# An attention and feed-forward kernel on one core: x loaded tile by tile behind its stores, and the work of heads 7 to 15 placed anew

## What is computed

```python
xn = layernorm(x)
q, k, v = (xn @ W + b for W, b in ((Wq, bq), (Wk, bk), (Wv, bv)))      # split into 16 heads
scores = q @ k.T / sqrt(32) + slope[head] * distances                  # causal
ctx = softmax(scores) @ v
gate, up = xn @ gate_w.T, xn @ up_w.T
out = x + ctx @ Wo + bo + (silu(gate) * up) @ down_w.T
```

## Time and profile before

| | |
|---|---|
| median of 3 runs | 791.17 us (789.69 to 795.04) |
| profiled execution | 789.27 us |
| its span, first to last instruction | 787.4 us |
| mean granted TensorE clock | 0.947 |
| busy: PE, DVE, ACT, POOL | 87%, 58%, 57%, 42% |
| attention part | about the first 475 us |

### The profile page before, as it was taken

The page is one execution under the profiler, slowest core; times in us unless marked ns, Lnnn a source line. Parts: engine busy times, 40 slices in busy tenths (PEclk is TensorE's granted clock), DMA queues, the critical chain, the costliest instruction groups (busy, mean ns, idle before and its releaser), DMA issues. The chain is left out here.

```text
span 787.4 us, 13689 instructions
## 1 busy us (share of the span) xinstructions
PE 686.6 (87%) x4884; PEld 550.2 (70%) x4884; DVE 459.0 (58%) x1290; ACT 445.2 (57%) x705; POOL 328.9 (42%) x191
## 2 busy tenths in 40 slices
PE   4888779989789898799997875698779999999997
PEld 3667567777668776677776653576658888888886
DVE  6277857879867798578787785555323223223112
ACT  4388867878767877688788822344332332232231
POOL 1555544544544645445455501222125235236334
PEclk9978999999899997999999996798998999999999
DMA  7886476475765466655659458558337565333101
GB/s 251 169 168 112 60 227 120 74 136 152 121 160 70 71 105 127 180 71 78 97 171 293 151 172 249 150 155 264 83 82 269 159 199 194 92 113 121 56 1 53
DMA packets 53067, 109.75 MB, mean 139 GB/s; under 512 B 6408, under 2 KB 6664, under 8 KB 51464
## 3 DMA queue, kind: packets, MB, share of 16 engines
q1 hardware_dynamic: 51416, 106.46, 54.7%
q10 hardware_dynamic: 1584, 2.43, 1.3%
HBM read 59.32 MB, written 25.17 MB: 107 GB/s over the span
## 5 line engine op out<-in xcount | busy, mean ns | idle before, releaser
L1131 POOL TENSOR_TENSOR work<-work 128x1280 f16<-128x1280 f32 x64 | 168.7, 2636 | 173.7 <-ACT work L1029 173.7
L1586 POOL TENSOR_TENSOR in_lo<-inner,in_hi 128x512 fp32r<-128x512 f32 x64 | 85.7, 1341 | 221.9 <-ACT in_hi L1502 221.9
L810 DVE CUSTOM_DVE_ANT_0 work<-bank,dist 128x128 f32<-128x128 f32 (+3 forms) x256 | 115.4, 487 | 78.9 <-PE bank L603 57.5
L1021 ACT ACTIVATE work<-work,neg_max 128x128 f32<-128x128 f32 (+3 forms) x256 | 129.4, 562 | 17.8 <-DVE neg_max L810 17.6
L1502 ACT CAST in_hi<-inner 128x512 fp32r<-128x512 f32 x64 | 39.9, 624 | 150.9 <-PE bank L1446 144.0
L1549 DVE TENSOR_TENSOR inner<-bank,silu 128x512 f32<-128x512 f32 x64 | 44.1, 689 | 136.4 <-ACT silu L1496 125.0
L617 PE MATMUL bank<-ident,work 128*128 128x128 f16 x1280 | 108.6, 230 | 10.1 <-DVE work L819 6.4
L1029 ACT CAST work<-work 128x1280 f16<-128x1280 f32 x64 | 80.7, 1261 | 56.2 <-PE bank L617 55.1
L617 PEld LDWEIGHTS bank<-ident,work 128*128 128x128 f16 x1280 | 78.1, 103 | 47.3 <-issue 33.5
L1444 PE MATMUL bank<-w_room,in_hi 128*128 128x512 f32 x256 | 102.5, 401 | 0.5 <-POOL in_lo L1586 0.5
L1445 PE MATMUL bank<-w_room,in_hi 128*128 128x512 f32 x256 | 102.2, 399 | 0.0
(11 more groups left out here) (100 smaller groups left out, 1303.5 us busy)
## 6 DMA issues: line engine op xcount, KB each, us to landing
q_stack<-parts SPq DMA_DIRECT2D x48, 256.0 KB, 5.7
k_stack<-parts SPq DMA_DIRECT2D x48, 256.0 KB, 6.2
z<-xt_scratch SPq DMA_DIRECT2D x128, 88.0 KB
x_in<-x SPq DMA_DIRECT2D x32, 256.0 KB, 4.1
xt_scratch<-xt_room SPq DMA_DIRECT2D x8, 1024.0 KB, 6.7
xt_room<-xt_scratch SPq DMA_DIRECT2D x6, 1024.0 KB, 10.9
factor<-c_basis SPq DMA_DIRECT2D x5, 1024.0 KB, 10.7
taps<-windows SPq DMA_DIRECT2D x5, 1024.0 KB, 8.4
```

The costliest lines, as they stand in the source:

```text
L810: dve.tensor_tensor_reduce(probs[:, s % 2, OFF[i]:OFF[i] + n], score_bank[i % 2][:, 0:n], dist[:, S - n:S], -slope(s), 3.4e38, ALU.add, AL ...
L1021: e = act.activation(tile, tile, ACT.Exp, bias=neg_max[:, s % 2, i:i + 1], scale=-1.0)
L1131: pool.tensor_tensor(probs16[:, s % 2, 1, :], probs[:, s % 2, :], probs16[:, s % 2, 0, :], ALU.subtract).then_inc(lo_ready, 1)
L1586: pool.tensor_tensor(in_lo[k % 2][:, :], inner[:, k % 2, :], in_hi[:, k % 2, :].bitcast(F32), ALU.subtract).then_inc(il_ready, 1)
```

## The change

Six things move, none is added or left out.

- SP loads a tile of the next batch's x as soon as that tile's own sum is stored, between the stores of the others (`room_for_x`). The first of these loads, for batch 1, stay where they were.
- The statistics of the next x go from DVE's steps 8 and 9 to steps 7 and 8, the inverse deviation and the normalization from 9 and 10 to 8 and 9, the turns of x on PE from 9 and 10 to 8 and 9.
- The split of v's last tile for heads 8 to 15 goes from step 7 to step 10.
- The turn of context 0 goes from step 7 to step 10, that of context 1 from 11 to 12.
- The projection of v's tile 0 goes from step 11 (where q's stands too) to step 10.
- In the last batch the mask's load is apart from `load_early`, which no longer waits for the last split of v.

The diff, cut to its core:

```diff
-         7: [("q", 3)], 8: [("k", 3)], 11: [("v", 0), ("q", 0)], 12: [("k", 0)], 13: [("v", 1), ("q", 1)],
+         7: [("q", 3)], 8: [("k", 3)], 10: [("v", 0)], 11: [("q", 0)], 12: [("k", 0)], 13: [("v", 1), ("q", 1)],
          14: [("v", 2)], 15: [("v", 3)]}
-TURNS = {2: [("c", 3)], 7: [("c", 0)], 9: [("x", 0), ("x", 1)], 10: [("x", 2), ("x", 3)], 11: [("c", 1)],
+TURNS = {2: [("c", 3)], 8: [("x", 0), ("x", 1)], 9: [("x", 2), ("x", 3)], 10: [("c", 0)], 12: [("c", 1)],
          15: [("c", 2)]}
-SPLITS = {13: [(0, 0)], 14: [(0, 1)], 1: [(0, 2)], 2: [(0, 3)], 4: [(1, 0)], 5: [(1, 1)], 6: [(1, 2)], 7: [(1, 3)]}
+SPLITS = {13: [(0, 0)], 14: [(0, 1)], 1: [(0, 2)], 2: [(0, 3)], 4: [(1, 0)], 5: [(1, 1)], 6: [(1, 2)], 10: [(1, 3)]}
...
-PJ_LAST = [("k", 3), ("c", 1), ("m", 0), ("m", 1), ("m", 2), ("c", 2), ("o", 0), ("o", 1), ("c", 3), ("o", 2), ("o", 3)]
+PJ_LAST = [("k", 3), ("c", 0), ("c", 1), ("m", 0), ("m", 1), ("m", 2), ("c", 2), ("o", 0), ("o", 1), ("c", 3), ("o", 2), ("o", 3)]
...
-                if carry and s == 9:
+                if carry and s == 8:
                     norm_apply(b + 1, 0)
                     norm_apply(b + 1, 1)
-                if carry and s == 10:
+                if carry and s == 9:
                     norm_apply(b + 1, 2)
                     norm_apply(b + 1, 3)
...
-                if carry and s in (8, 9):
-                    norm_stats(b + 1, (2 * s - 16, 2 * s - 15))
+                if s == HALF - 1 and b < B - 1:
+                    norm_stats(b + 1, (0, 1))
+                if carry and s == HALF:
+                    norm_stats(b + 1, (2, 3))
                 for half, t in SPLITS.get(s, []):
-                    if s >= HALF:
+                    if s >= HALF and half == 0:
...
+            def room_for_x(b, q):
+                sp.wait_ge(res_st[q], 16 * b)
+                sp.nop(nofuse=True)
+                if b < B - 1:
+                    load_x(b + 1, q)
...
-                for q in range(1, QT):
-                    store_sum(b - 1, q)
                 for q in range(QT):
-                    sp.wait_ge(res_st[q], 16 * b)
-                sp.nop(nofuse=True)
+                    if q:
+                        store_sum(b - 1, q)
+                    if q > 1:
+                        room_for_x(b, q - 2)
+                for q in range(2, QT):
+                    room_for_x(b, q)
...
             sp.wait_ge(pj_full, pj_total(("k", KC - 1), B - 1))
+            load_early(sp)
             sp.wait_ge(v_done, 2 * QT * B)
-            load_early(sp)
+            load_mask(sp)
```

More of the change, by code:

```diff
@@ L305, in load_early, with load_mask @@
                 sp.dma_start(taps[c][:], cpts[c]).then_inc(chunk_ld[c], 16)
+        def load_mask(sp):
             sp.dma_start(mask.bitcast(U32).rearrange("p g n -> p (g n)"), c_mask).then_inc(mask_ld, 16)
@@ L379, in build_kernel @@
                   (wq, wk, wv, wo), bq, bk, bv, c_dist, c_ident, c_scale, x_t, xt_d, mid_d, base,
-                  (load_basis, load_early, load_pieces, load_windows, load_moments, copy_across),
+                  (load_basis, load_early, load_mask, load_pieces, load_windows, load_moments, copy_across),
                   (taps_op, taps_high, taps_low), bm_early, (bme_ld, pad_st, mom_sv), mom_d)
@@ L430 @@
 MOMENTS = {12: 0, 13: 1, 14: 2}
-PJ_LAST = [("k", 3), ("c", 1), ("m", 0), ("m", 1), ("m", 2), ("c", 2), ("o", 0), ("o", 1), ("c", 3), ("o", 2), ("o", 3)]
-PJ_LAST_ENDS = [("k", 3), ("c", 1), ("m", 0), ("m", 1), ("m", 2), ("c", 2), ("c", 3)] + [("o", t) for t in range(QT)]
-CARRIED = [("k", 3)] + [("c", c) for c in range(1, KC)] + [("o", t) for t in range(QT)] + [
+PJ_LAST = [("k", 3), ("c", 0), ("c", 1), ("m", 0), ("m", 1), ("m", 2), ("c", 2), ("o", 0), ("o", 1), ("c", 3), ("o", 2), ("o", 3)]
+PJ_LAST_ENDS = [("k", 3), ("c", 0), ("c", 1), ("m", 0), ("m", 1), ("m", 2), ("c", 2), ("c", 3)] + [("o", t) for t in range(QT)]
+CARRIED = [("k", 3)] + [("c", c) for c in range(KC)] + [("o", t) for t in range(QT)] + [
     ("m", m) for m in range(3)]
@@ L474, in attention @@
               c_dist, c_ident, c_scale, x_t, xt_d, mid_d, base, loads, blends, bm_early, early, mom_d):
-    load_basis, load_early, load_pieces, load_windows, load_moments, copy_across = loads
+    load_basis, load_early, load_mask, load_pieces, load_windows, load_moments, copy_across = loads
     taps_op, taps_high, taps_low = blends
@@ L1059, in step @@
                         v_high(b + 1, half, t)
-                    elif s < HALF - 1:
+                    elif s < HALF - 1 or half:
                         v_high(b, half, t)
@@ L1135, in step @@
                 halved = back(b, s, 1)
-                if carry and s in (9, 10):
-                    inverse_std(b + 1, s - 9)
+                if carry and s in (8, 9):
+                    inverse_std(b + 1, s - 8)
                 if halved:
@@ L1228, in _ @@
             stack(0, 2)
+            for t in range(QT):
+                load_x(1, t)
             for b in range(1, B):
-                for t in range(QT):
-                    load_x(b, t)
                 stack(b - 1, 3)
```

## The result

The changed kernel takes 804.9 us (median of 4 runs, 804.38 to 807.18), the kernel before 792.0 beside it on the same chip: a ratio of 1.0205, with a 95% interval of 1.0166 to 1.0244. It is slower, by about 2%. Forecast were 792.0 and a range of 778 to 801. The profiled execution has a span of 803.2 us where the one before had 787.4, 15.8 more.

The account below looks back on a forecast made before the run. PE, busy 87%, was taken as the bound, with some 10 us per batch of waits open to better spreading. 789.27 - 3.9 (intervals) + 0.8 (last batch) + 3.9 (clock) = 790.1, as a median 792.0; range 778 to 801.

Parts of the forecast that it names:

- Where the 10 us per batch lie: Head 8 to next batch's head 8 lasts 107.53 us, PE busy 97.50; waits in heads 8, 9 and step 11.
- Loads of x: SP's queue: tile 1's load goes right behind the last store; DVE's wait for it taken as 0.
- rival D: Tile 1 of x lands late for DVE's statistics: +3.7 us in two batches, 799.4; chance 0.05.
- Steps 10 and 11, the hold of the split: DVE's split of v, held by POOL's 2.65 us subtraction, ends at 8.6; interval 10.3 us against 7.89, unheld 8.0.
- Step 9, the pair of normalizations: DVE has two normalizations (1.48 us) and two low halves of x, no statistics: interval 8.2 us against 7.37.
- Step 8: DVE loses context 0's low half (0.60 us), gains two normalizations (1.48): interval 6.59 becomes 7.5.
- The clock: PE's half clock after the new wait for the split: 1.3 us per batch (0 to 3.1), 3.9 in all.
- rival C: Two slow-clock spells per batch on PE, in steps 10 and 11: 6.2 us lost, median 806.7; chance 0.12.
- Steps 11 to 13: Intervals 5.6 for 11.77, 6.0 for 5.61, 8.7 for 8.38 us, the last by DVE's split pushed past POOL's start.
- The last batch: Added DVE work hidden up to 1.9 us by PE's stack wait; context 1's turn comes behind: +0.8, 0 to +2.7.

Follow-up runs that it names:

- the last run: x's loads wait for all four stores again, against the kernel with the split in DVE's gap and POOL's two waits (0.9878): ratio 0.9964.
- the run with the gap and two waits: Changed kernel, v's split in DVE's idle gap of step 10, POOL waiting for four normalizations and step 8's context multiplication: 0.9878, 778.9 us beside 790.3.

## Why the prediction was wrong

*Where the 10 us per batch lie*: right. What the change would get of them unheld was 43.7 us per batch between heads 8 and 14 by the prediction; 42.8 were measured in two batches and 45.1 in one, with the long holds taken away and the split in another place.

*Loads of x*: right. Tile 1 went out at 191.21, right behind the last store of 190.80 (by then the whole kernel was 4.7 us later), and landed 3.4 us later, just as DVE came to it. No wait came, and rival D did not happen. Left as it was, the load order would have cost the new place of the statistics some 5 us, as the last run shows.

*Steps 10 and 11, the hold of the split*: right to 0.2 us. The cast began 5.49 us behind the third score matmul and ended at 8.07, where 8.2 had been said, the last piece at 8.53 (8.6), three batches out of three. The rule of the Trainium skill (SBUF — State Buffer, "SBUF: two separate sides") that the pair is an exclusive lock for the whole instruction agrees with these traces: 0.29 us became 2.58, 0.17 became 2.30.

*Step 9, the pair of normalizations*: here the prediction failed. It said "the pair of normalizations 1.48", as at 201.57, where one of POOL's subtractions, of 1.3 us, had overlapped it. In its new place it is met by two, the second of 2.64 us: 3.77, in all three batches, 2.3 us more than priced. I had placed POOL against DVE for the split, where the diff puts an operation in a new place, and taken over a duration for an operation that was moved just as much. The earlier trace rows held the warning: 1.48 for two operations of 0.5 is already a hold, and a hold is a property of the place and not of the operation. The run in which POOL waits for the pair took 1.6% off. This was the largest term that was mis-sized, 6.9 us in three batches.

*Step 8*: 7.88 in place of 7.5. The context's multiplication is held (1.23 us for 0.35), which was in no term, while the pair of this step took 0.99 where 1.48 had been put in. The difference of the two is the 0.4.

*The clock*: here the prediction had the size wrong too. Its term was 1.3 us per batch, while what happened is what rival C describes, two spells in every batch. In the second they run from 209.06 to 215.89 and from 222.72 to 229.54. The first stretches the scores and v's projection of step 10 from 2.04 to 3.41 us; by the intervals the second costs 1.4 in step 10's end and 0.7 in step 11. That is 3.5 us in this batch, and about 5 more than the term of 3.9 in the three.

That C's 806.7 came near the measured 804.9 is luck: its price of 6.2 us per batch was about twice what the spells cost, and the hold of step 9, which C had not, made up for it. The Trainium skill (TensorE: Matmul & The Clock Gate, "Part 1: The HAM clock gate") has the slow clock as the state that an idle PE falls back to, and from this the prediction drew that each new wait would be followed by a spell. The traces agree for the wait of 3.15 us, which one followed in all three batches, but not for each wait: that of 2.30 in the first batch of the kernel before was followed by none, its window having kept 1.00:

```profile
90.94 0.85 PE L603 MATMUL bank<-k_stack,q_stack 96*128 96x384 f32 x2 [2.30 <-DVE neg_max L810]
```

Waits of 1.4 and 1.75 us in steps 8 and 9 had a spell behind them in all three batches of the run in which POOL waits for the pair, waits of 1.19 and 1.75 none in two batches of the run with the gap and two waits.

*Steps 11 to 13*: 6.34, 5.99 and 8.38 for 5.6, 6.0 and 8.7. The 0.3 for the split pushed by context 1's low half did not come.

*The last batch*: 2.4 in place of 0.8, inside its bounds of 0 to 2.7. The 1.9 us of cover at the stack gave way, because the stack itself landed later (10.2 us for 8.8) and PE waited 2.68 for it, in spite of a wait of 1.22 for the split ahead of it:

```profile
435.51 0.20 PE L636 MATMUL bank<-v_parts,work 128*128 128x98 bf16 x1 [1.22 <-issue]
...
441.37 0.77 PE L605 MATMUL bank<-k_stack,q_stack 96*128 96x256 f32 x2 [2.68 <-issue]
```

*The sum.* The three batches missed the forecast intervals by 5.3, 6.2 and 5.5 us, 17.0, of which 3.9 had been put in for the clock; the last batch missed by 1.6. That makes 14.7 on the forecast span of 788.2: 802.9, beside 803.2 measured. By the trace of the second batch the 6.2 are 2.3 of held normalizations, 3.5 of half clock and 0.4 of step 8. In all, the 14.7 are 6.9 of held normalizations, some 5 of half clock beyond what was put in, 1.2 of step 8 and 1.6 of the last batch.

*The range* ended at 801 because C was left out at 0.12. C alone would not have been enough: with the pair at 1.48 and the spells still there, the run in which POOL waits for the pair measured 1.0047, which beside 792.0 is 796 us and inside the range. It took the hold of step 9 as well, which no rival had. Nor did that hold bring the first spell, since the spell came in all three batches of the run without the hold.

What stays open: what decides whether a spell follows a wait, and why the last stack landed 1.4 us later than before. In the runs its last copy lands 8.3 to 11.3 us after issue, so the 1.4 may be no more than the scatter of single executions.

## What to carry to other kernels

When two engines can block each other, lay both timelines side by side for every operation that is moved, and for those left in place whose neighbour is moved; a duration read at one place is no price for another. Half a microsecond decides over the whole length of the other engine's instruction, and such ties fall differently from batch to batch. The cure that worked is a wait on the side that has slack: GpSimd waited 0.8 us for two short DVE operations and PE got 2.6 to 3.0 us back, while starting GpSimd earlier only moved the hold to a tiny operation on the critical path.

## What the runs showed of the hardware

- An addition on 128x2 elements took 2.30 us behind a GpSimd subtraction of 2.61. The price of this hold was the rest of the other's length, not the size of what was held.
- Held were the cast, `tensor_scalar` out of SBUF into SBUF (128x2 and 128x512), and subtractions or multiplications with both inputs in SBUF. Not held beside the same subtractions were copies and subtractions with an input in PSUM (0.55, 0.64 us), `neg_max` and the aggregation of statistics (0.25 for two).
- The held cast ended 0.15 to 0.16 us behind GpSimd's end, in all three batches.
- The hold went the other way too: a GpSimd subtraction that began while a DVE normalization ran took 2.90 us for 2.64.
- 17 score matmuls more per batch, laid into waits, did not slow the kernel (0.9834 for 0.9878 and 0.9796 for 0.9851, both with overlapping intervals), and no low spell came in steps 8 to 15 of any of the six batches, where two of six had some without them. The same 58 matmuls took 5.73 us of PE at a granted clock of 1.00 and 8.59 at 0.68.
